# Sage layers of a graph network as dense products with a matrix of edge counts

## The reference

```
mlp:   h = elu([x[src], edge] @ W1a + b1a) @ W1b + b1b;  mean of h over the edges of a target;  second small net
gat:   two attention layers: softmax over the edges of each target (and a loop), weighted sum of (x @ W)[src]
sage:  three layers:  h = relu(h @ Ws + (sum of h[src] over the edges of a target / degree) @ Wn + b)
pool:  m = x[src] + edge;  per-feature softmax over the edges of a target, with maxima;  sum, small net
```

## Time and profile before

| | |
|---|---|
| time, median of 3 runs (lowest, highest) | 4086.49 us (4083.54, 4086.62) |
| span of the profiled execution | 4084.8 us |
| busy: PE, DVE, ACT, POOL | 57%, 53%, 45%, 65% |
| mean clock granted to TensorE | 0.69 of full |
| indirect gathers on POOL | 2787 |
| DMA, mean over the span | 122 GB/s |

### The profile page before, as it was taken

The page is one execution under the profiler, slowest core; times in us unless marked ns, Lnnn a source line. Parts: engine busy times, 40 slices in busy tenths (PEclk is TensorE's granted clock), DMA queues, the critical chain, the costliest instruction groups (busy, mean ns, idle before and its releaser), DMA issues.

```text
span 4084.8 us, 45091 instructions
## 1 busy us (share of the span) xinstructions
PE 2340.4 (57%) x10010; PEld 1833.9 (45%) x10010; DVE 2167.9 (53%) x5164; ACT 1837.8 (45%) x4303; POOL 2646.4 (65%) x2793
## 2 busy tenths in 40 slices
PE   6777785344442444444555566655755555477776
PEld 5665653334342434442333354443544344365554
DVE  6888873556565555554222233333434444666668
ACT  3887874334332434335343344334253432444443
POOL 4777712777753777744777727777467776577771
PEclk8999997555556555555555577778855555788886
DMA  6555512333322334324655523333267777455551
GB/s 194 158 161 155 161 54 52 81 84 82 82 58 59 81 77 84 77 48 112 159 158 158 158 85 105 106 105 105 64 187 209 213 212 199 125 155 155 156 159 41
DMA packets 589398, 497.69 MB, mean 122 GB/s; under 512 B 73851, under 2 KB 530608, under 8 KB 588800
## 3 DMA queue, kind: packets, MB, share of 16 engines
q0 software_dynamic: 101696, 235.14, 23.1%
q1 hardware_dynamic: 484630, 254.57, 22.5%
q10 hardware_dynamic: 2828, 5.18, 0.4%
HBM read 426.04 MB, written 68.57 MB: 121 GB/s over the span
## 4 chain that ended last, share of the span: by engine, by line
POOL 51%; issue 19%; PE 12%; DVE 11%; DMA 4%; DVEq 1%; ACT 1%; POOLq 0%; SPq 0%; ACTq 0%
POOL big L597 24%; POOL big L610 18%; POOL y_and_h L624 9%; PE ps L744 5%; DVE y_and_h L1395 3%; DMA big<-table_sage,src_block 2%; DVE ps L1387 2%; PE ps L666 2%; DVE big L1367 2%; PE ps L895 1%; PE ps L680 1%; PE ps L892 1%; DVEq L418 1%; DVEq L1387 1%; DVE x_sb L1500 1%
## 5 line engine op out<-in xcount | busy, mean ns | idle before, releaser
L597 POOL DMA_INDIRECT big<-table_sage,src_block x1173 | 1109.5, 946 | 550.3 <-issue 347.2
L610 POOL DMA_INDIRECT big<-table_gat,src_idx x832 | 787.1, 946 | 479.6 <-issue 247.5
L1367 DVE TENSOR_TENSOR big<-big,ps 128x257 f32 (+3 forms) x1664 | 591.8, 356 | 219.1 <-issue 15.9
L624 POOL DMA_INDIRECT y_and_h<-table_pool,src_block x391 | 377.7, 966 | 166.7 <-issue 118.9
L597 POOL DMA_INDIRECT big<-table_mlp,src_block x391 | 371.3, 950 | 159.8 <-issue 117.4
L1154 ACT ACTIVATE rows<-iota,dst_rel 128x128 f32<-128x128 f32 x768 | 243.7, 388 | 260.2 <-PE ps L895 172.3
L1367 DVE TENSOR_TENSOR y_and_h<-y_and_h,ps 128x256 f32 x416 | 175.0, 421 | 338.9 <-PE ps L892 293.4
L1176 ACT ACTIVATE y_and_h<-y_and_h 128x128 f32<-128x128 f32 (+1 forms) x26 | 8.0, 309 | 677.0 <-DVE y_and_h L1607 677.0
L744 PE MATMUL ps<-w_sb,ea_sb 128*128 128x256 f32 x832 | 213.0, 400 | 126.8 <-DVE y_and_h L1395 115.6
L1798 DVE TENSOR_TENSOR_SCAN big<-ps,big 128x512 f32<-128x512 f32 x98 | 125.4, 1280 | 282.5 <-PE ps L921 279.6
L1849 DVE TENSOR_TENSOR_SCAN ps<-ps,small,big 128x512 f32<-128x512 f32 (+1 forms) x98 | 126.3, 1289 | 252.9 <-PE ps L921 209.0
(11 more groups left out here) (302 smaller groups left out, 5643.8 us busy)
## 6 DMA issues: line engine op xcount, KB each, us to landing
big<-in_ea_blocks SPq DMA_DIRECT2D x194, 256.0 KB, 4.1
ea_sb<-in_ea_blocks SPq DMA_DIRECT2D x416, 64.0 KB
ea_sb<-rel_rows SPq DMA_DIRECT2D x208, 128.0 KB
prefix_blocks<-big SPq DMA_DIRECT2D x97, 256.0 KB, 2.5
big<-prefix_blocks SPq DMA_DIRECT2D x97, 256.0 KB, 4.1
below_blocks<-big SPq DMA_DIRECT2D x97, 256.0 KB, 2.7
rows<-in_ea_rows SPq DMA_DIRECT2D x97, 256.0 KB
big<-table_sage,src_block POOLq DMA_INDIRECT x1173, 2.8
```

The costliest lines, as they stand in the source:

```text
L597: pool.indirect_dma_start(ring[:, (block + RING_FIRST[k]) % (n * G), :], None, table[k], bass.IndirectOffsetOnAxis(src_block[:, block:bloc ...
L610: pool.indirect_dma_start(ring[:, step % GAT_RING, :], None, table[k], bass.IndirectOffsetOnAxis(src_idx[:, step:step + 1], 0))\
L624: pool.indirect_dma_start(pool_rows[q][:, i, :], None, table["pool"], bass.IndirectOffsetOnAxis(src_block[:, block:block + 1], 0)).then_in ...
L1367: dve.tensor_tensor(to, to, bank_of(j), ALU.add).then_inc(accumulated, 1)
```

## The change

The sum of `h[src]` over the edges of a target, for all targets, is a product of the node rows with a matrix of counts: the entry at (source, target) is the number of edges between the two. The change builds this matrix in DRAM (`cells`, 3328 x 3328 float32) and multiplies by it.

- In the mlp pass SP stores zeros into the cells, one store of 128 x 832 float32 with each of the 104 groups.
- An edge's cell has the number source x 3328 + target (`make_keys`). Where two edges of a block have the same cell, only one of them may add. `find_equal` compares the keys of an edge block with each other on VectorE (128 x 512 for four blocks), `sum_equal` sums the comparisons on TensorE, and `place_counts` gives the first edge the count and the others a spare cell. It is done for 31 of 98 sets of four blocks in mlp and 67 in gat1. SP loads the keys spread over the partitions (`load_keys`).
- POOL adds the counts with 391 indirect DMAs that add in DRAM (`add_counts`), in four streams: an add waits until the last one of its stream has landed. A target that lies across the border of two streams has an extra column for the later one. 112 adds stand after mlp's gathers, 70 among gat1's (one a group from group 34), 66 after them, 85 among gat2's (from group 10), 58 after them.
- Each sage sum is `dense_sum`: 25 tiles of 128 source rows by 3140 columns, loaded by SP into four buffers (`load_cells`); for each tile TensorE multiplies its 128 x 128 node rows by seven chunks of up to 512 columns, and the sums stay in seven PSUM banks. sage1 takes two such sums. Each sum after the first starts with the four tiles that the last left in the buffers. `scale_sums` divides by the degree and adds the extra columns. The third sum is turned back into rows (`sT`).
- Both sweeps over the edge features move: the upward one beside gat1, the downward one beside gat2, one scan a group (`find_prefix`, `find_maximum`), with four buffers. What is stored is now the maximum itself, and the last stage subtracts it (`subtract_maxima` there in place of one addition).
- The gathers, tables, one-hot matrices and sums of the three sage passes go.

The core of the diff:

```diff
+COUNTED = [("mlp", 0, 31, 60), ("gat1", 31, 54, 11), ("gat1", 54, 76, 37), ("gat1", 76, 98, 62)]
+SCATTERED = {"after mlp": 112, "gat1": 70, "after gat1": 66, "gat2": 85}
+FIRST_SCATTER_SLOT = {"gat1": 34, "gat2": 10}
...
+            for g in range(NG):
+                load_ea(g, g % 2, edge_product, 0)
+                sp.dma_start(cell_units[g], zero_cells).then_inc(cleared, 16)
+                load_keys("mlp", g)
...
+            def add_counts(times):
+                for _ in range(min(times, NB - scatters[0])):
+                    i, q = divmod(scatters[0], STREAMS)
+                    block = q * PER_STREAM + i
+                    if scatters[0] == 0:
+                        pool.wait_ge(cleared, 16 * NG)
+                    pool.wait_ge(cells_ready, 1 + sum(i >= end for _, _, end, _ in COUNTED))
+                    if i:
+                        pool.wait_ge(scattered[q], 16 * i)
+                    pool.indirect_dma_start(cells, bass.IndirectOffsetOnAxis(cell_of_edge[:, block:block + 1], 0),
+                                            count_of_edge[:, block:block + 1], None, compute_op=ALU.add)\
+                        .then_inc(scattered[q], 16)
+                    scatters[0] += 1
...
             gather_blocks("mlp", pre_ready, 0, LAG)
+            add_counts(SCATTERED["after mlp"])
             gather_steps("gat1")
+            add_counts(SCATTERED["after gat1"])
             gather_steps("gat2")
-            gather_blocks("sage0", summed, base["sage0"], LAG)
-            gather_blocks("sage1", summed, base["sage1"], LAG)
-            gather_blocks("sage2", summed, base["sage2"], LAG)
+            add_counts(NB)
             gather_rows_of_pool()
...
+            def dense_sum(n, rows_of):
+                for u in range(SRC_TILES):
+                    a, slot = tile_of(n, u), slot_of(n, u)
+                    m, last = P if a < SRC_TILES - 1 else LAST_ROWS, u == SRC_TILES - 1
+                    pe.wait_ge(cells_loaded[slot], 16 * loads_of_slot(n, u))
+                    for k, c in enumerate(SUM_ORDER):
+                        at = chunk_columns(c, CELLS_USED)
+                        if u == 0 and n:
+                            pe.wait_ge(chunk_read, CHUNKS * (n - 1) + k + 1)
+                        mm = pe.matmul(ps[:, c, 0:at.stop - at.start], rows_of(a)[0:m, :], cell_ring[slot][0:m, at],
+                                       start=u == 0, stop=last)
+                        if last:
+                            mm.then_inc(chunk_done, 1)
+                    if not last:
+                        mm.then_inc(tile_summed, 1)
+                    unit = own_unit_at(n, u)
+                    if unit is not None:
+                        if OWN_BEFORE[n] + unit:
+                            pe.wait_ge(self_read, OWN_BEFORE[n] + unit)
+                        (row_self_term if n == 3 else column_self_term)(n, unit)
...
+            def spread_borders(k, i):
+                if k == "gat1":
+                    j, kind = i, 0
+                    pe.wait_ge(*(prefix_done, i) if i else (cells_ready, 1))
...
+            def find_equal(k, g):
+                for of, i0, i1, at in COUNTED:
+                    i = i0 + g - at
+                    if of == k and i0 <= i < i1:
+                        dve.wait_ge(key_loaded[i % 2], 16 * (i // 2 + 1))
+                        if i >= 2:
+                            dve.wait_ge(equal_summed, i - 1)
+                        own = by_stream(key_col[:, :])[:, :, i].unsqueeze(2).to_broadcast([P, STREAMS, P])
+                        dve.tensor_tensor(equal[i % 2], key_spread[k][i % 2], own, ALU.is_equal).then_inc(equal_ready, 1)
...
                     if WEIGH <= q < NG + WEIGH:
                         weigh(q - WEIGH)
+                    if 1 <= q <= NBG:
+                        (find_prefix if k == "gat1" else find_maximum)(q - 1)
+                    find_equal(k, q)
                     if q + 1 < NG:
                         mark_nodes(q + 1)
```

More of the change, by code:

```diff
@@ L755, in sum_hidden, with sum_equal @@
                 mm.then_inc(summed, 1)
+            def sum_equal(k, g):
+                for batch, (of, i0, i1, at) in enumerate(COUNTED):
+                    i = i0 + g - at - SUMMED_AFTER[of]
+                    if of == k and i0 <= i < i1:
+                        pe.wait_ge(equal_ready, i + 1)
+                        if batch:
+                            pe.wait_ge(cells_ready, batch)
+                        for q in range(STREAMS):
+                            mm = pe.matmul(counts_bank(k, i1 - i0)[:, i - i0, q, :], equal[i % 2][:, q, :], powers[:, :],
+                                           start=True, stop=True)
+                        mm.then_inc(equal_summed, 1)
             pe.wait_ge(read_by["dve"], fills_read(FIRST_FILL["flag"], "dve"))
@@ new lines, in column_self_term @@
+            def column_self_term(n, unit):
+                c, m = divmod(unit, 2)
+                at = slice(c * COLS, (c + 1) * COLS)
+                terms = [(weight("Ws0", 0, m * P, P), xT)] if n == 0 else \
+                    [(weight("Ws1", k, m * P, P), big[:, 4 + k, :]) for k in range(2)]
+                for k, (w, of) in enumerate(terms):
+                    mm = pe.matmul(ps[:, 7, 0:COLS], w, of[:, at], start=(k == 0), stop=(k == len(terms) - 1))
+                mm.then_inc(self_done, 1)
@@ L1358, in zero, with accumulate @@
                 dve.wait_ge(acc_zeroed, PASSES.index(k) + 1)
-            def adding(k, g, tiles, bank_of, acc):
-                def add(j):
+            def accumulate(k, g, tiles, bank_of, acc, order=range(G)):
+                for n, j in enumerate(order):
                     to = acc(tiles[j])
-                    done = sums_before(k) + G * g + j
-                    if not (isinstance(done, int) and done == 0):
+                    done = sums_before(k) + G * g + n
+                    if done:
                         dve.wait_ge(accumulated, done)
+                    if j == G - 1:
+                        place_counts(k, g)
                     dve.tensor_tensor(to, to, bank_of(j), ALU.add).then_inc(accumulated, 1)
-                return add
-            def accumulate(k, g, tiles, bank_of, acc):
-                add = adding(k, g, tiles, bank_of, acc)
-                for j in range(G):
-                    add(j)
             dve.wait_ge(rows_stored, 192)
@@ new lines, in place_counts @@
+            def place_counts(k, g):
+                for of, i0, i1, at in COUNTED:
+                    if of != k or g != at + i1 - 1 - i0 + SUMMED_AFTER[of]:
+                        continue
+                    dve.wait_ge(equal_summed, i1)
+                    found = counts_bank(k, i1 - i0).rearrange("p i q m -> p q i m")
+                    cell, to, n = (by_stream(a)[:, :, i0:i1] for a in (target_col, cell_of_edge, count_of_edge))
+                    for q in range(STREAMS):
+                        ins = dve.tensor_scalar(n[:, q, :], cell[:, q, :], -1.0, spare_cells[:, q:q + 1], ALU.mult, ALU.add)
+                    link(ins)
+                    link(dve.scalar_tensor_tensor(n, found[:, :, :, 1], twice, n, ALU.is_gt, ALU.mult))
+                    link(dve.tensor_tensor(to, n, cell, ALU.add))
+                    dve.tensor_copy(n, found[:, :, :, 0]).then_inc(cells_ready, 1)
@@ L1423, in _ @@
                     split_bias()
+                if g == NG // 2 + 4:
+                    make_keys()
+                find_equal("mlp", g)
                 if g < NG:
@@ L1812, in _, with join_own @@
+            def join_own(m):
+                for c in range(CHUNKS):
+                    at = chunk_columns(c, SUMMED_NODES)
+                    dve.tensor_tensor(big[:, 2 + m, at], big[:, 4 + m, at], big[:, 2 + m, at], ALU.add).then_inc(own_joined, 1)
+            dve.memset(big[:, 0, SUMMED_NODES:NODES], 0.0)
+            for unit in range(2 * NCOL):
+                add_own_bias(0, unit)
+            dve.wait_ge(inverses_moved, 32)
+            scale_sums(0)
             dve.wait_ge(self_read, 2 * NCOL)
@@ L1948, in lay_out @@
     src_blocks = np.ascontiguousarray(src[:NB * P].reshape(NB, P).T)
+    dst_all = np.full(n, PAD_NODE, np.int32)
+    dst_all[:N_EDGES] = a["dst"]
+    pairs = np.ascontiguousarray(np.stack([src.reshape(-1, P), dst_all.reshape(-1, P)]).transpose(2, 0, 1))
+    borders = np.array([[-1] + [dst_all[q * PER_STREAM * P - 1] for q in range(1, STREAMS)]], np.int32)
     dst = np.full(n + 2, PAD_NODE, np.int32)
```

698 lines of the change are left out of this document (347 added, 351 removed).

## The result

The changed kernel takes 3704.7 us (median of 4 runs, 3700.3 to 3707.2) where the kernel before took 4086.6 on the same chip: a ratio of 0.9065, with a 95% interval of 0.9052 to 0.9078. Faster, as forecast with 0.94, but 310 us above the forecast of 3395 and 85 above the range, whose upper end was 3620.

What follows compares the result with a forecast made beforehand. POOL's gathers with their issue were taken to bound most passes, VectorE the message pass's end. A stretch of 1707.5 us becomes 772 (935 less), 243 is added, net 692: span 3393, plus 1.7 gives 3395 us; range 3335 to 3620.

Steps and rivals of the forecast that it cites:

- step 2: The first 112 indirect adds, before gat1: 1.25 us each, bounds 0.95 to 2.5; gat1's first gather 48 us later.
- The landings: POOL waits in each of four streams for its last add to land; gathers land in 2.8 us, at most 5.5.
- First add: After the message pass, waiting for the last zeroing store: 561.7 + 21 + 0.5 + landing 2.8 = 586.
- First burst: 112 adds on POOL between the message pass and gat1, at 1.25 us each: 140 us.
- The rival of scans and sums that wait for each other: In both attention passes VectorE's scans wait for TensorE's spread borders: +134 and +115 us, 3644 in all; chance 0.09.
- Pause: 66 adds on POOL between gat1 and gat2: 82.5 us in a pause of 81.4, so +1.
- Last gather to first dense product: After gat2: 58 adds 72.5 us, landing 3, then the first cell tile with its latency; 83 us.
- Dense sums: Four sums of 25 tiles on TensorE, 596 us, plus 60 for the work between them: 656 us.
- End: From the last dense sum's first scaling to the pool gather: 33 us, where it was 30.5 before.
- The adds are dearer: POOL, 391 adds in series: 3884 us at 2.5 us each, slower from 3.02; chance 0.12 for 1.4 to 3.0, 0.05 above.
- Crowded queues: Message pass: zeroing stores crowd the DMA queues, 30 us more, 3479 with slow cell loads; chance 0.06 for both.
- The shared port: gat1: each VectorE comparison takes its 0.64 us from POOL, pass 43 us longer, 3438 in all; chance 0.03.

Runs made afterwards that it cites:

- whole counts: Changed kernel with plain writes for adds, keys also compared with the column before (97 more comparisons): 3496 us, ratio 0.8561; with zeroing stores moved ahead, 4376 on another chip.
- early zeroing: Zeroing stores moved ahead, four in every three groups: changed kernel with its adds 4056 us, with plain writes of full counts 4376, same chip.

## Why the prediction missed

**The step that failed is step 2, the price of an add.** It took 1.25 us, the pitch of a gather, "the row that it is nearest to"; it is 1.93. The prediction had the bounds (0.95 to 2.5) and the formula, 3395 + 391 (x - 1.25), which at 1.93 gives 3661: 266 of the 310 us. It failed in two ways. It argued that a gather goes by its descriptors whatever their bytes, true of gathers and small plain writes alike, and let that stand for an instruction that no row showed. And the range, cut at x = 1.8, left out a value well inside the bounds, at a chance of 0.12 for 1.4 to 3.0. The landings that were named as what would make adds dear cost 16.0 us in 18 waits.

Point by point, measured against forecast:

- First add 605.0 against 586: +19. The stores, costed at nothing with a bound of 30, are 17 of it; comparisons and key loads (12 against 14) were right.
- First burst 220.2 us against 140: +80. An add was at its cheapest here, with a mean of 1.58: 112 x (1.58 + 0.30 - 1.25) = 71, and one landing wait of 9.0 us.
- gat1 668.7 against 607.5: +61; 70 x 0.70 = 49, and gathers of 0.97 us. POOL bound it, as said; VectorE held it up for 2.1 us in both passes. The rival of scans and sums that wait for each other did not come.
- Pause 130.1 against 82.5: +48, all of it adds: the pause had room for 81 us, and 66 adds at the true price need 127. The pause could hide no more than its own length.
- gat2 690.8 against 626: +65, of which 85 x 0.68 = 58.
- Last gather to first dense product 122.2 against 83: +39, 58 x 0.68.
- Dense sums 645.3 against 656: -11. A sum is 147.6 us (2437.0 to 2584.6) and the part up to the second sum's first product 41.0 against 42. TensorE is the bound, the loads are hidden, the clock is at its upper level. The Trainium skill ("TensorE: Matmul & The Clock Gate", "HAM oscillation") names waiting on DMA as what loses the clock; here TensorE stood idle for 50.4 us until the first tile was there, and the first 4 us of products ran at a granted clock of 0.50; after that it waited for no tile, and from 2445 us to the end of the first sum the clock was 1.00. The trace agrees with the page in both.
- End 31.6 against 33; last pass and tail 591.2 against 578: +13. The pass has no instruction more, but its gathers take a mean of 996 ns instead of 965: 391 x 0.031 = 12.

These add to 313 us, the distance between 3705.1 and 3393 and a rounding. The price of the adds and their landings is about 274 of it. Most of the rest is the stores' 17, 12 in the last pass, and dearer gathers in the attention passes, 11 and 5, less the 12 by which the dense sums and the end came in under their forecast.

**The rivals.** "The adds are dearer" is what happened, at x = 1.93 and far from the 3.02 at which it would have lost. "Crowded queues" came in part. The shared port came small: 0.09 us for each comparison, twice the 0.04 that I had from the row, and not 0.64. The Trainium skill ("SBUF — State Buffer", in "Who interferes with whom") has a VectorE operation with two SBUF inputs contend with a GpSimd instruction that reads SBUF. Taken at the operation's full length, as my prediction took it, that would have cost gat1 45 us; without the comparisons both passes' gathers together were 6 us shorter, so the measurement decides against the full length. The same section also tells of a probe in which such an operation did not stall a GpSimd DMA, which I had passed over, and the 6 us are near that.

## What to carry to other kernels

An operation that no row shows is not priced by its likeness to one that a row shows, if it does one thing more: where hundreds of them stand in series, keep both bounds in the range, and measure one. Then ask what the dear part is, and whether an engine with time left can do it: the sum that the DMA made at 0.6 us an add cost VectorE one comparison of some 0.68 us for every four adds. That pays only where POOL is the bound. It won 208 us on the chip of 4083 us and lost some 320 where VectorE had waits of its own, so a time from one chip is not yet a verdict. And a cover is used up once: a pause of 81 us hides 65 operations at 1.25 us and only 42 at 1.93.

## What the runs showed of the hardware

- An adding indirect DMA of 128 4-byte rows holds POOL for 1.57 us (median; mean 1.63), a plain write for 0.97, a gather for 0.94, each with 0.30 of issue behind it. With 64 rows the add takes 1.41 and the write 0.90.
- In the last pass VectorE has two operations a group with both inputs in SBUF, before and after. A gather's mean lies 18 ns above its median of 947 before and 49 ns after; only the order of the operations behind the gather's landing has changed. So it seems to be the moment at which they fall beside a gather that counts; no run took that apart.
- Chips differed: the kernel before took 4083 us on one and 4966 to 4989 on others, where VectorE and ScalarE had waits of up to 57 us for a queue that the trace does not identify. The order of two kernels turned with that: whole counts against adds is 3496 against 3705 us on the one kind, and 4376 against 4056 (both with early zeroing) on the other.
